# Recurrent step of a four-layer graph network: the one-hot copy and one transposition change place, and stores are split

## The reference, cut to what matters

```python
x = x + L1_ffn(layernorm(x)[None], W_f, b_f, W_i, b_i, W_c, b_c, W_o, b_o)[0]
# W_f, W_i, W_c, W_o are (1024, 512): rows 0..511 take the input, rows 512..1023 the state h
# for t in range(625): gates = [x_t, h] @ W + b
#   f, i, o = sigmoid(...), g = tanh(...);  c = f * c + i * g;  h = o * tanh(c);  out[t] = h
```

## Time and profile before

| what | value |
|---|---|
| median of 3 runs | 4727.78 us |
| time of the profiled execution | 4735.63 us |
| its span, first to last instruction | 4733.9 us |
| busy: PE, PEld, DVE, ACT, POOL | 94%, 46%, 49%, 38%, 8% |
| chain that ended last, by engine | PE 83%, DVE 8%, ACT 5%, issue 3%, DMA 1% |

### The profile page before, as it was taken

How to read it: one execution, slowest core, us unless ns; L and a number is a source line. 1 busy time by engine, 2 the same in 40 slices (tenths; PEclk the granted TensorE clock), 3 DMA queues, 4 the chain that set the end, 5 groups by cost and what they waited for, 6 DMA issues and landing times.

```text
span 4733.9 us, 136928 instructions
## 1 busy us (share of the span) xinstructions
PE 4430.5 (94%) x53052; PEld 2175.6 (46%) x53052; DVE 2338.7 (49%) x10628; ACT 1799.4 (38%) x7133; POOL 361.7 (8%) x351
## 2 busy tenths in 40 slices
PE   9878898899999999999999999899989998799998
PEld 7445554344444333444444333333346745555554
DVE  6324314566666666666666666566632524611111
ACT  0010111566666444666666444444431511111111
POOL 0000001000000222000000221012210001000000
PEclk9998899999999999999999999999998989789999
DMA  2000102520000000000000000000003312011111
GB/s 70 27 31 28 43 27 84 168 89 0 9 0 0 2 2 4 1 0 0 0 0 1 2 2 5 0 1 1 1 25 79 73 37 74 30 45 63 62 55 37
DMA packets 49386, 139.42 MB, mean 29 GB/s; under 512 B 25236, under 2 KB 33195, under 8 KB 37911
## 3 DMA queue, kind: packets, MB, share of 16 engines
q1 hardware_dynamic: 39065, 113.72, 7.2%
q0 software_dynamic: 10208, 24.08, 2.6%
HBM read 114.92 MB, written 22.60 MB: 29 GB/s over the span
## 4 chain that ended last, share of the span: by engine, by line
PE 83%; DVE 8%; ACT 5%; issue 3%; DMA 1%; POOL 0%; DVEq 0%; ACTq 0%; POOLq 0%
PE PS L1001 38%; PE PS L719 31%; PE PS L995 5%; PE PS L1057 3%; DVE ls_turn L1971 3%; PE PS L805 2%; ACT ls_th L1399 2%; ACT ls_gate L1392 1%; DVE ls_pr L1979 1%; DMA gate_inputs<-BUF 1%; PE PS L750 1%; PE PS L1135 1%; ACT picked L1408 1%; PE PS L1185 1%; PE PS L1125 1%
## 5 line engine op out<-in xcount | busy, mean ns | idle before, releaser
L1001 PE MATMUL PS<-BUF,ls_hid 128*1 128x256 f32 x40000 | 2272.1, 379 | 0.0
L1001 PEld LDWEIGHTS PS<-BUF,ls_hid 128*1 128x1 f32 x40000 | 930.4, 84 | 1096.1 <-DVE ls_hid L1998 141.5
L1971 DVE STREAM_TRANSPOSE ls_turn<-PS 128x192 f32<-128x192 f32 x1250 | 474.2, 379 | 515.1 <-PE PS L1001 515.1
L1399 ACT ACTIVATE ls_th<-ls_pr 128x1 f32<-128x1 f32 x2500 | 600.4, 287 | 144.8 <-DVE ls_pr L1979 35.0
L719 PE MATMUL PS<-ring,BUF 128*125 128x512 f32 (+1 forms) x1440 | 619.2, 589 | 23.1 <-DVE BUF L1722 5.8
L719 PE MATMUL PS<-BUF,ring 128*128 128x512 f32 (+1 forms) x2176 | 599.2, 437 | 2.3 <-ACT BUF L1280 1.4
L1392 ACT ACTIVATE ls_gate<-ls_turn 128x6 f32<-128x6 f32 x1250 | 265.4, 212 | 826.8 <-DVE ls_turn L1971 826.8
L1998 DVE SCALAR_TENSOR_TENSOR ls_hid<-ls_gate,ls_th 128x1 f32<-128x1 f32 x2500 | 371.5, 160 | 250.3 <-ACT ls_th L1399 214.8
L719 PEld LDWEIGHTS PS<-BUF,ring 128*128 128x128 f32 x2176 | 332.4, 192 | 275.8 <-issue 273.7
L719 PEld LDWEIGHTS PS<-ring,BUF 128*125 128x125 f32 x1440 | 270.6, 190 | 352.8 <-issue 333.1
L1288 ACT ACTIVATE BUF<-PS,cols 128x625 f32<-128x625 f32 x130 | 101.5, 782 | 625.4 <-PE PS L719 622.5
(11 more groups left out here) (311 smaller groups left out, 3073.8 us busy)
## 6 DMA issues: line engine op xcount, KB each, us to landing
cell_bias<-BUF SPq DMA_DIRECT2D x5, 2441.4 KB
BUF<-cell_bias POOLq DMA_DIRECT2D x5, 2441.4 KB, 14.8
ring<-in_L_wo SPq DMA_DIRECT2D x11, 1024.0 KB, 4.8
ring<-in_L_wi SPq DMA_DIRECT2D x8, 1024.0 KB, 4.9
ring<-in_L_wg SPq DMA_DIRECT2D x8, 1024.0 KB, 4.8
ring<-in_L_wout SPq DMA_DIRECT2D x8, 1024.0 KB, 4.8
gate_inputs<-BUF SPq DMA_DIRECT2D x5, 1500.0 KB
BUF<-in_L_wh SPq DMA_DIRECT2D x4, 1024.0 KB, 12.8
```

Of the source, the lines that this page charges most:

```text
L1001: ins = nc.tensor.matmul(ls_sum[u][f][32 * q:32 * q + 1, :].rearrange("p (j n) -> p j n", j=4), ls_hid[:, c:c + 1], ls_half[:, q, c, :, f, :],
L1399: nc.scalar.activation(ls_th[:, f, c:c + 1], ls_pr[:, f, c:c + 1], ACT.Tanh, scale=0.5, bias=ls_pr[:, f, 2 + c:3 + c]).then_inc(ls_tanh[f], 1)
L1971: V.transpose(ls_turn[:, f, 2:8, :], ls_sum[u][f][:, 64:256].rearrange("p (g n) -> p g n", g=6)).then_inc(ls_turned[f], 1)
```

## The change

Five edits, most of them in the order of the instructions:

1. ACT: the copy of the next one-hot column moves from between the halves to the start of the step, in front of the first tanh. It now waits for `ls_full[0]` of the same step, since then the seeds that read `picked` are done.
2. DVE: the transpositions of half 1 are taken apart. The 192-column one stands right behind the first h chunk, then comes the second h chunk, and then the 64-column one.
3. PE: add(1,0), which needs only h chunk 0, moves in front of the wait for chunk 1.
4. SP: each store of 125 partitions becomes two, of 112 and 13 partitions. The result is stored row tile by row tile as DVE finishes each (10 transfers in place of 1).
5. DVE: the clearing of the accumulators moves into the loop over the gate-input tiles, behind tiles 16 and 18.

```diff
+ROW_SPLIT = ((0, 112), (112, R))
...
-                        sp.dma_start(gx_d[t * R:(t + 1) * R, :, :], gx_parts[t % 2][0:R, :, :]).then_inc(gx_out[t % 2], 16)
+                        for a, b in ROW_SPLIT:
+                            sp.dma_start(gx_d[t * R + a:t * R + b, :, :], gx_parts[t % 2][a:b, :, :]
+                                         ).then_inc(gx_out[t % 2], 16)
...
-            sp.wait_ge(*half_done(last))
-            sp.dma_start(io["out"].rearrange("(t p) f -> p t f", p=R), X[0:R, :, :]).then_inc(out_done, 16)
-            sp.wait_ge(out_done, 16)
+            for t in range(NT):
+                sp.wait_ge(*evacd("L3f.y7", t))
+                for a, b in ROW_SPLIT:
+                    sp.dma_start(io["out"][t * R + a:t * R + b, :], X[a:b, t, :]).then_inc(out_done, 16)
+            sp.wait_ge(out_done, 32 * NT)
...
                     add(0, 0)
+                    add(1, 0)
                     pe.wait_ge(ls_h[0], t * 2 + 2)
                     add(0, 1)
-                    add(1, 0)
...
                 def pick_step(t):
+                    act.wait_ge(ls_full[0], t)
                     nc.scalar.activation(picked[:, :], pick[:, bass.ds(t, 1)], ACT.Copy).then_inc(ls_picked, 1)

                 def step(t, last=False):
+                    if not last:
+                        pick_step(t + 1)
                     gates(0, t)
                     cell(0, t)
-                    if not last:
-                        pick_step(t + 1)
                     gates(1, t)
...
+                    home = (first["L1f.gx"][0] + i) % SLOTS
+                    if i >= 4 * NT - SLOTS and home % 2 == 0:
+                        dve.wait_ge(*evacd("L1f.gx", i))
+                        for f in range(2):
+                            V.memset(ls_sum[home // 2][f], 0.0).then_inc(ls_blank, 1)
...
                     turn(0, t, u)
+                    turn_o(0, t, u)
                     product(0, t)
                     cell(0, t)
-                    hidden(0, t)
+                    hidden(0, 0, t)
                     turn(1, t, u)
+                    hidden(0, 1, t)
+                    turn_o(1, t, u)
                     halve(0, t)
```

More of the change, by code:

```diff
@@ L537, in gate_inputs @@
                         sp.wait_ge(*made("L1f.gxlow", 4 * t + 4))
[L538 removed]
+                        for a, b in ROW_SPLIT:
+                            sp.dma_start(gx_d[t * R + a:t * R + b, :, :], gx_parts[t % 2][a:b, :, :]
+                                         ).then_inc(gx_out[t % 2], 16)
                         if t == 0:
[L540 removed]
+                            sp.wait_ge(gx_out[0], 32)
                             for g in range(3):
                                 gx_load(sp, g, gx_first)
[L543 to L544 removed]
+                    sp.wait_ge(gx_out[0], 96)
+                    sp.wait_ge(gx_out[1], 64)
                     for g in range(3, GX_HOMES):
@@ L668, in _ @@
                 pool.wait_ge(pad_out, 32)
-                pool.wait_ge(gx_out[0], 48)
-                pool.wait_ge(gx_out[1], 32)
+                pool.wait_ge(gx_out[0], 96)
+                pool.wait_ge(gx_out[1], 64)
                 pool.wait_ge(ls_turned[1], GX_FROM[2] + 2)
@@ L1375, in _ @@
                     if t >= 2 and j == 0:
-                        act.wait_ge(gx_out[t % 2], 16 * (t // 2))
+                        act.wait_ge(gx_out[t % 2], 32 * (t // 2))
                     act.wait_ge(*evacd("L1f.gx", i))
@@ L1418, in _ @@
                 act.wait_ge(*made("sort.consts"))
-                pick_step(0)
+                nc.scalar.activation(picked[:, :], pick[:, 0:1], ACT.Copy).then_inc(ls_picked, 1)
                 def rank_far(i):
@@ L1972, in turn, with turn_o @@
                                 ).then_inc(ls_turned[f], 1)
+                def turn_o(f, t, u):
+                    dve.wait_ge(ls_full[f], t + 1)
                     V.transpose(ls_turn[:, f, 0:2, :], ls_sum[u][f][:, 0:64].rearrange("p (g n) -> p g n", g=2)
@@ L1989, in halve, with hidden @@
                     V.tensor_scalar(ls_gate[:, f, 6:8], ls_c[:, f, :], 0.5, None, ALU.mult).then_inc(ls_state[f], 1)
-                def hidden(f, t):
-                    dve.wait_ge(ls_out_gate[f], t + 1)
-                    if f == 0:
+                def hidden(f, c, t):
+                    if c == 0:
+                        dve.wait_ge(ls_out_gate[f], t + 1)
+                    if (f, c) == (0, 0):
                         dve.wait_ge(ls_kept, t + 1)
                         dve.wait_ge(ls_used, t + 1)
-                    for c in range(2):
-                        dve.wait_ge(ls_tanh[f], t * 2 + (c + 1))
-                        V.scalar_tensor_tensor(ls_hid[:, 2 * f + c:2 * f + c + 1], ls_gate[:, f, 8 + c:9 + c], 1.0,
-                                               ls_th[:, f, c:c + 1], ALU.add, ALU.mult).then_inc(ls_h[f], 1)
+                    dve.wait_ge(ls_tanh[f], t * 2 + (c + 1))
+                    V.scalar_tensor_tensor(ls_hid[:, 2 * f + c:2 * f + c + 1], ls_gate[:, f, 8 + c:9 + c], 1.0,
+                                           ls_th[:, f, c:c + 1], ALU.add, ALU.mult).then_inc(ls_h[f], 1)
                 def step(t, u, between=None):
                     turn(0, t, u)
+                    turn_o(0, t, u)
                     product(0, t)
                     cell(0, t)
-                    hidden(0, t)
+                    hidden(0, 0, t)
                     turn(1, t, u)
+                    hidden(0, 1, t)
+                    turn_o(1, t, u)
                     halve(0, t)
@@ L2011, in step @@
                         between()
-                    hidden(1, t)
+                    hidden(1, 0, t)
+                    hidden(1, 1, t)
                     halve(1, t)
-                for u in range(2):
-                    for f in range(2):
-                        V.memset(ls_sum[u][f], 0.0).then_inc(ls_blank, 1)
                 def rank_pass(k, t0):
```

## The result

The changed kernel takes 4645.48 us (median of 4 runs, 4644.77 to 4647.12), the kernel before, run beside it, 4727.32 us. The ratio is 0.9828 with a 95% interval of 0.9816 to 0.984, so it is faster by 81.8 us, or 1.7%. Forecast were 4654.4, 73.4 us less than before. One execution among the experiments (of e_no_c2) took 15342 us at a granted clock of 0.45 and is left out of that kernel's time.

A forecast was written before the change was run, and what follows sets the result against it. PE's recurrent matmuls bound the kernel, with the one-hot copy and h chunk 2 tied in free steps. Step 48.8 + gate inputs and clock 15.3 + result's store 9.3 = 73.4 us less, to 4654.4 us, range 4628 to 4685.

The forecast's parts named there:

- The copy: Free step, ACT and PE: one-hot copy at step start costs nothing; first h matmuls at 1.43, 0.27 us earlier.
- The transpositions: Free step, DVE: half-1 transposition at 1.30 and not 1.45, 0.15 us earlier; product not moved; chunk 2 at 2.60.
- The new step: Free steps: h chunk 2 becomes the limit, 3.95 us in place of 4.11; 48.8 us less over 305 steps.
- The steps with the sort: The 320 steps with the sort's matmuls: PE is last there, not the copy, so gain 0.
- Rival D: The sort's steps gain too: 22 us more, 4632 us; chance 0.08.
- The gate inputs: Gate-input stage: split stores hide behind PE, the clearing and base matmuls under the last tile's run-out; gain 13.8 us.
- the clock term: First recurrent step: after only 3.4 us of idling PE has the full clock, another 1.5 us gained.
- The result's store: End of kernel, SP: row tiles stored early, so the last store takes 2.0 us; gain 9.3 us.
- A: Rival, scatter steps: the later halving is held by POOL, product 1.2 us later in 240 steps; 4943 us; chance 0.05.
- B: Rival, free steps: DVE instructions do not overlap, product 0.21 us later, step 4.16 us; 4718 us; chance 0.06.
- C: Rival, free steps: h chunk 2 is no limit, step 3.85 us; 4621 us; chance 0.08.
- E: Rival: the recurrence gains nothing, only the stores do; 4703 us; chance 0.07.

The follow-up runs named there:

- e_no_c2: Changed kernel with PE multiplying fixed zero columns in place of h chunks 2 and 3, without waiting for them; 4614.7 us, run again for its trace 4612.08 us.
- e_turn: Kernel before with only DVE's transpositions of half 1 taken apart; 4723.29 us, ratio 0.9994.
- e_loop: Kernel before with the three edits of the recurrent step (ACT, PE, DVE), stores and clearing as before; 4675.05 us, ratio 0.9885.
- e_add_back: Changed kernel with add(1,0) back behind add(0,1); 4646.97 us, ratio 0.9833.
- e_stores: Kernel before with only the split gate-input stores and the result stored by row tiles, clearing and steps as before; 4706.46 us, ratio 0.9958.
- e_pick: Kernel before with only the one-hot copy at the step's start and add(1,0) ahead of the wait for chunk 1; 4710.59 us, ratio 0.9969.
- e_slip: Changed kernel with an extra 64-column transposition on DVE ahead of half 1's, delaying the halving; 4645.62 and 4654.18 us, ratio 0.984.
- e_96_29: Changed kernel with gate-input stores split into 96 and 29 partitions, not 112 and 13; 4672.47 us, ratio 0.9876.

## Why the prediction was right, and where its sizes were off

*The copy (right in mechanism, one link time too long).* It costs nothing at T, the seeds come at 1.04, chunk 0 is late next. But the first h matmuls start at 1.40 and not 1.43. The figure I took from chunk to matmul, 0.21 to 0.25, is 0.215 in every kernel here; my upper end came of adding the 0.04 between a load and its matmul to the load's start, in rows where the load that is shown is already the late one.

*The transpositions (right).* Half 1's at 1.30, the halving 0.51 behind it with 0.12, the product at 0.66 (forecast 0.65), chunk 2 at 2.60, as worked out. e_turn shows the 0.15, and that it is worth nothing by itself.

*The new step (the term that was mis-sized).* Forecast 3.95, measured 3.926 with a scatter and 3.878 without. In the sum 2.84 + 0.65 + 0.47 it is the 2.84: chunk 2 at 2.60 lets add(0,2) start at 2.815. The 65 steps without a scatter have the product at 0.16, so chunk 2 at 2.55; I named that and did not price it. The term of 48.8 us came out at 57.8. By steps it would be 240 x 0.188 + 65 x 0.236 = 60.5; 2.3 of the missing 2.7 lie in two steps that were longer after than before, step 499 (4.66 us, before 4.11) and step 538 (5.47, before 4.13). The stretches of step 538, before and after:

```profile
3132.10:3136.20 4.10, 2.68 (x56) 1.27 (x60) 2.25 (x16) 2.07 (x11) 1.20 (x1) 1.00 0.00 0
```

```profile
3077.10:3082.60 5.50, 4.49 (x56) 1.80 (x60) 2.23 (x16) 2.21 (x11) 1.19 (x1) 0.69 0.03 1
```

The granted clock is 1.00 before and 0.69 after, and in step 499 1.00 and 0.85. Step 499 takes its 3.88 in e_loop and e_add_back, and step 538 takes 5.28 in e_stores, whose steps are those of before, so neither belongs to the edits of the step. That the edits need one another was foreseen in "the two are tied"; e_pick and e_turn show the tie to be 0.04 loose.

*The steps with the sort (right).* 4.184 before and after. Rival D is out.

*The gate inputs (13.8 right within 1.2, the clock term wrong).* Measured 12.6. The store is hidden, the stage is PE's 68.68 us in one piece, and from its end to the seeds there are 862.87 - 859.54 = 3.3 us (forecast 3.4). The missing 1.2 is about what the stage's first tile started later in this execution: 790.86, and in the profile before

```profile
789.26 20.62 PE PS L719 x48
```

which is 1.6 ahead; in e_loop, which has the gate-input stage of before, that tile starts at 791.54, so this start varies by itself. Counted from that tile the stage got 14.2 us shorter, against 13.8. The seeds came at 862.87, where 861 to 862 was named. The further 1.5 us, a full clock in the first step, did not come: 5.14 us for 64 rows against 3.46. The stretches around it:

```profile
860.00:863.00 3.00, 0.88 (x12) 0.58 (x14) 2.90 (x6) 1.95 (x4) 0.62 (x1) 1.00 0.35 92
863.00:867.20 4.20, 4.20 (x56) 1.61 (x52) 0.57 (x3) 1.64 (x2) 0.00 (x0) 0.59 0.80 262
```

PE was busy 0.88 of 3.00 us at the full clock (2.4 GHz), and then 4.2 us of the first step ran at a mean of 0.59, that is for the most part at 1.2 GHz, about as long as after 15 us of idling before (0.60). I had argued from the length of the idle time; the rows show no such relation.

*The result's store (right).* Forecast 2.0 for the last wait and a gain of 9.3, measured 1.5 and, at the end of the span, 9.3.

*Sum.* 57.8 + 12.6 + 9.3 = 79.7 of 81.8 us; 2.1 are not placed. The forecast of 73.4 had the step's term 9.0 too small and the start 2.7 too large. The two errors offset each other in part, which is luck.

*The rivals.* A is out: the halving is not held where the change puts it, nor in e_slip (0.64 behind the transposition, 0.05 ahead of POOL). B, no overlap on DVE, is out: the 64-column transposition starts at 1785.45, 0.08 ahead of the end of the chunk's instruction (1785.41 + 0.12). The strict form of the Trainium skill's sentence ("VectorE: DVE Perf Modes", section "The DRAIN you can't avoid") does not hold here, by these rows; the same section's exception, that an instruction which is not held starts earlier, is compatible with them. C, chunk 2 no limit, is out for the changed kernel, and its step would have been 3.81 (e_no_c2_again) where I wrote 3.85. E is out, and so is the store that doesn't spread, though e_96_29 shows what a split with a prime part costs.

## What to carry to other kernels

In a loop where two producers feed one engine almost at once, moving either alone gives little (15.7 and 3.0 us here) and both together much (51 to 60); so work out the second limit ahead of judging the first edit. Put the numbers of a chain from one fixed event, in the kernel's own rows, and look up the short link times (0.215 from chunk to matmul) in a row where the load really waits. When a loop is tightened, look at what else is released inside it: moving POOL's issue out of the product's way by one semaphore gave another 12 to 13 us. And before a transfer is split, count how each part divides: SP's longest wait for a gate-input store was 12.8 us for 125 partitions, 5.8 for 112 + 13 and 17.9 for 96 + 29.

## What the runs showed of the hardware that was not expected

- The granted clock fell for the first 4.2 us of the recurrence (0.59) although PE had worked 0.88 of the 3 us ahead of it, and had been at the full clock for 68 us before that. In steps 499 and 538 it was 0.85 and 0.69 in the trace of after and 1.00 in that of before.
- POOL's issue of an indirect transfer lasts 1.17 us. A DVE product that starts 0.01 ahead of it takes 0.21 and not 0.16. A halving that starts 0.05 ahead keeps its 0.12, and one that starts 0.11 to 0.53 behind takes its 0.16; one that starts 0.82 behind is held to 0.03 ahead of POOL's end. The cell, the h chunks (0.16 each) and the 192-column transposition (0.38) that run inside the issue are not held. What decides is open.
- Executions of one kernel differ by some 9 us by the granted clock behind the recurrence (0.93 to 0.95), with four kernels on both levels. A difference of that size between two single runs says nothing.
